# FFN input turned as fp32 halves and scaled out of PSUM, with VectorE's clips ahead of the product of their slot

## The reference

```
x = x + tanh(g_ffn) * FFN(layernorm(x))
FFN(x):
  scale = sigmoid(clip_x) * max|x| / 127          # one number for the whole tensor
  xq    = clip(round(x / scale), -128, 127) * scale
  gate  = xq @ wq(w_gate).T ;  up = xq @ wq(w_up).T     # 704 columns each, weights quantised by row
  h     = silu(gate) * up
  h     = clip(round(h / s2), -128, 127) * s2     # s2 from max|h|, again one number
  return h @ wq(w_down).T
```

## Time and profile before

| what | us |
|---|---|
| median of 3 runs | 591.95 (591.29 to 592.18) |
| profiled execution | 591.61 |
| its span | 589.7 |
| PE busy | 561.8 (95%) |
| DVE busy | 534.1 (91%) |
| ACT busy | 444.0 (75%) |
| POOL busy | 241.7 (41%) |

### The profile page before, as it was taken

The page is one execution under the profiler, slowest core; times in us unless marked ns, Lnnn a source line. Parts: engine busy times, 40 slices in busy tenths (PEclk is TensorE's granted clock), DMA queues, the critical chain, the costliest instruction groups (busy, mean ns, idle before and its releaser), DMA issues. The chain is left out here.

```text
span 589.7 us, 18094 instructions
## 1 busy us (share of the span) xinstructions
PE 561.8 (95%) x6585; PEld 262.7 (45%) x6590; DVE 534.1 (91%) x690; ACT 444.0 (75%) x871; POOL 241.7 (41%) x366
## 2 busy tenths in 40 slices
PE   8999999998999999999999999999999999888985
PEld 4555655233434444444444444444444433433364
DVE  4999999999999999999999899899899885799988
ACT  2667776277787897897897897897797762887694
POOL 3799998702211344562333224214215211555400
PEclk9999999999999999999999999999999999999999
DMA  7579873432122212221221231132121000000024
GB/s 278 195 254 338 283 225 132 144 97 86 56 73 75 76 55 75 79 62 57 80 79 54 66 95 54 54 90 72 54 79 33 2 2 0 2 1 1 0 108 179
DMA packets 29902, 55.21 MB, mean 94 GB/s; under 512 B 5544, under 2 KB 19752, under 8 KB 29864
## 3 DMA queue, kind: packets, MB, share of 16 engines
q1 hardware_dynamic: 29864, 54.71, 28.9%
HBM read 37.62 MB, written 16.78 MB: 92 GB/s over the span
## 5 line engine op out<-in xcount | busy, mean ns | idle before, releaser
L929 ACT ACTIVATE prob<-st_ps 128x512 f32<-128x512 f32 x512 | 280.6, 597 | 61.7 <-PE st_ps L787 54.4
L787 PE MATMUL st_ps<-q,k 98*32 98x512 bf16 x2048 | 178.5, 380 | 1.9 <-ACT prob L929 1.9
L989 DVE TENSOR_REDUCE negm<-xT_ps 128x2 f32<-128x1024 f32 x128 | 154.4, 1206 | 7.3 <-PE xT_ps L339 6.8
L989 DVE TENSOR_REDUCE negm<-v_ps 128x2 f32<-128x1024 f32 x128 | 154.2, 1205 | 3.8 <-PE v_ps L339 3.8
L811 PE MATMUL pv_ps<-prob,v_u 128*32 128x512 f32 x1024 | 132.6, 592 | 0.6 <-ACT prob L929 0.3
L787 PEld LDWEIGHTS st_ps<-q,k 98*32 98x32 bf16 x2048 | 57.3, 95 | 90.5 <-ACT prob L929 33.7
L1181 POOL TENSOR_TENSOR msplit<-negm,onesf 128x16 bf16<-128x16 f32 x32 | 7.1, 221 | 205.9 <-DVE negm L989 205.9
L339 PE MATMUL xT_ps<-k,q 96*32 96x512 bf16 x1024 | 78.5, 379 | 1.1 <-DVE negm L989 1.0
L339 PE MATMUL v_ps<-k,q 96*32 96x512 bf16 x1024 | 78.1, 380 | 1.3 <-DVE negm L989 0.9
L339 PEld LDWEIGHTS xT_ps<-k,q 96*32 96x32 bf16 x1024 | 27.1, 96 | 36.4 <-issue 13.2
L811 PEld LDWEIGHTS pv_ps<-prob,v_u 128*32 128x32 f32 x1024 | 31.2, 110 | 26.8 <-issue 2.8
(11 more groups left out here) (155 smaller groups left out, 782.3 us busy)
## 6 DMA issues: line engine op xcount, KB each, us to landing
qk_parts<-parts SPq DMA_DIRECT2D x32, 384.0 KB, 3.2
k<-qk_parts SPq DMA_DIRECT2D x32, 192.0 KB
q<-qk_parts SPq DMA_DIRECT2D x32, 192.0 KB
ctx<-in_ctxT SPq DMA_DIRECT2D x8, 512.0 KB, 4.6
X<-in_x SPq DMA_DIRECT2D x8, 512.0 KB, 6.2
k<-qk_parts SPq DMA_DIRECT2D x32, 128.0 KB
q<-qk_parts SPq DMA_DIRECT2D x32, 128.0 KB
out<-X SPq DMA_DIRECT2D x7, 512.0 KB, 2.6
```

Source lines behind the costliest of these rows:

```text
L787: last = nc.tensor.matmul(score_bank(i)[lo:lo + COLS, :], k6[g][:, h, kt * P + lo:kt * P + lo + COLS], q6[g][:, h, :], start=True, stop=True)
L929: nc.scalar.activation(prob[kt % 2][:, h, :], score_bank(HPU * kt + h)[:], ACT.Exp, scale=SCALE).then_inc(exp_done, 1)
L989: nc.vector.tensor_reduce(negm[g % 2][:, lo:lo + 2], pair[:], op=ALU.max, axis=AX.X, negate=True).then_inc(mx_read, 1)
```

## The change

Each chunk is now transposed before it is scaled: PE turns `V` itself, in fp32, by halves of the 256 values, 4 transposes of 128 x 128 per half into bank 7 (512 fp32, the whole bank). One pass of ACT (half 0) or DVE (half 1) multiplies by 1/scale and writes int16, from PSUM to SBUF; one clip of DVE over both halves, int16 to bf16, writes `xqT` straight. `scale_x` out of SBUF, `keep_chunk` and `xq` are gone. PE turns half 1 of chunk 1 after slot 0, the halves of the next chunk 0 after slots 3 and 6, half 0 of the next chunk 1 after slot 9. ACT scales in slots 3 and 9 behind its copy of up (in slot 9 that is ahead of silu 10); DVE scales ahead of its products of slots 0 and 5 and clips ahead of those of slots 1 and 7. In pair 0 the four halves go to banks 6, 5, 7 and 2, the first two without a wait for the scale; 3 fillers follow where 9 were. On PE the pairs are written out, not a loop.

```diff
-START, END_A, ..., TO_SCALE, TO_DOWN, TO_CLIP, TO_TURN = 8, 2, 2, 10, 24, 9, 17, 10, 4
+START, END_A, ..., TO_SCALE, TO_DOWN, TO_CLIP, TO_TURN = 8, 2, 2, 10, 24, 3, 17, 10, 4
 # PE
-def transpose_first(): ...
-def transpose_chunk(p, k): ...
+def turn(bank, n, h):
+    for t in range(4):
+        last = nc.tensor.transpose(bank[:, t * P:(t + 1) * P], V[:, 4 * n + t, h * P:(h + 1) * P], ident[:])
+    return last
+def turn_first():
+    for k in range(2):
+        if k:
+            pe.wait_ge(gmax_ready, 1)
+        for h in range(KC):
+            last = turn(first_banks[k][h], k, h)
+        last.then_inc(first_turned, 1)
+def turn_half(n, h):
+    if h:
+        pe.wait_ge(x_kept[0], n - 1)
+    elif n == 2:
+        pe.wait_ge(first_kept[1], 2)
+    else:
+        pe.wait_ge(x_kept[1], n - 2)
+    turn(xT_bank, n, h).then_inc(x_turned, 1)
 ...
-                pe.wait_ge(xqT_kept[0], p)          # at slot 0
+            pe.wait_ge(xq_ready, 2 * p + 1)
+        if is_start(p) and s == 2:
+            pe.wait_ge(first_kept[1], 2)
         if s == NI:
-            pe.wait_ge(xqT_kept[1], p + 1)
+            pe.wait_ge(xq_ready, 2 * p + 2)
 ...
-        if s == 1:
-            transpose_chunk(p, 1)
-        if s == 7 and not last_pair(p):
-            transpose_chunk(p + 1, 0)
+        if s == 0 and not is_start(p):
+            turn_half(2 * p + 1, 1)
+        if not last_pair(p):
+            if s in (3, 6):
+                turn_half(2 * p + 2, (s - 3) // 3)
+            if s == 9:
+                turn_half(2 * p + 3, 0)
 spread(0)
+turn_first()
 stay_busy(banks[:, 0, :], TO_SCALE)
-transpose_first()
-over_pairs(pe, body)
+for p in range(PAIRS):
+    body(p)
 # ACT
-        if s == 7 and not last_pair(p):
-            keep_chunk(p + 1)
+        if s in (3, 9) and not last_pair(p):
+            scale_half(2 * p + 2 + s // 9, s // 9)
+def scale_half(n, k):
+    act.wait_ge(x_turned, 2 * n - 3)
+    act.wait_ge(xq_ready, n - 1)
+    nc.scalar.activation(xi[k][:, 0, :], xT_bank, ACT.Copy, scale=ainv[:, 0:1]).then_inc(x_kept[0], 1)
 # DVE
-def scale_x(p, k): ...
-def keep_chunk(p): ...
+def scale_half(n, k):
+    dve.wait_ge(x_turned, 2 * n - 2)
+    nc.vector.tensor_scalar(xi[k][:, 1, :], xT_bank, ainv[:, 0:1], None, ALU.mult).then_inc(x_kept[1], 1)
+def clip_x(n, k):
+    ...                                             # waits for both halves
+    nc.vector.tensor_scalar(xqT[k], xi[k], QMAX, -QMAX - 1.0, ALU.min, ALU.max).then_inc(xq_ready, 1)
 for s, (ck, c) in enumerate(SLOT):
+    if s == 0 and not is_start(p):
+        scale_half(2 * p + 1, 1)
+    if s == 1 and not is_start(p):
+        clip_x(2 * p + 1, 1)
+    if s == 5 and not last_pair(p):
+        scale_half(2 * p + 2, 0)
+    if s == 7 and not last_pair(p):
+        clip_x(2 * p + 2, 0)
     ...                                             # product and maximum of the slot
-    if s == 2:
-        keep_chunk(p)
-    if not last_pair(p):
-        if s in (2, 6):
-            scale_x(p + 1, s // 4)
-        if s in (3, 7):
-            clip_x(p + 1, s // 4)
```

More of the change, by code:

```diff
@@ L343, in build @@
         CONSTS = 5
-        START, END_A, PROLOGUE, TO_PROJECT, TO_FFN, TO_SCALE, TO_DOWN, TO_CLIP, TO_TURN = 8, 2, 2, 10, 24, 9, 17, 10, 4
+        START, END_A, PROLOGUE, TO_PROJECT, TO_FFN, TO_SCALE, TO_DOWN, TO_CLIP, TO_TURN = 8, 2, 2, 10, 24, 3, 17, 10, 4
         with nc.Block() as block:
@@ L1301, in build @@
         sil = [wf_flat[:, 512 * i:512 * (i + 1)] for i in range(UR)]
-        xi = [wf_flat[:, 2048 + 512 * i:2048 + 512 * (i + 1)].bitcast(I16).rearrange("p (t d) -> p t d", t=4) for i in range(2)]
-        xq = [wf_flat[:, 3072 + 512 * i:3072 + 512 * (i + 1)].bitcast(BF16).rearrange("p (t d) -> p t d", t=4) for i in range(2)]
+        xi = [wf_flat[:, 2048 + 512 * i:2048 + 512 * (i + 1)].bitcast(I16).rearrange("p (c t) -> p c t", c=KC) for i in range(2)]
         xqT = [wfq_flat[:, 1024 * i:1024 * (i + 1)].rearrange("p (c t) -> p c t", c=KC) for i in range(2)]
@@ L1313, in build @@
         u_ps = [banks[:, GR + i, :] for i in range(UR)]
-        xqT_ps = banks[:, 7, :].bitcast(BF16).rearrange("p (c t) -> p c t", c=KC)
-        xqT0_ps = [banks[:, 7 - c, 0:256].bitcast(BF16) for c in range(KC)]
+        xT_bank = banks[:, 7, :]
+        first_banks = [[banks[:, i, :] for i in (6, 5)], [banks[:, i, :] for i in (7, 2)]]
         spread_ps = banks[:, 7, 0:P]
@@ L1322, in build @@
         ascale_ready = sem("ascale_ready")
-        xs_ready = sem("xs_ready")
-        xs0_ready = [sem(f"xs0_ready{k}") for k in range(2)]
         xq_ready = sem("xq_ready")
[L1326 to L1330, removed]
+        first_turned = sem("first_turned")
+        first_kept = [sem(f"first_kept{k}") for k in range(2)]
+        x_turned = sem("x_turned")
+        x_kept = [sem(f"x_kept{h}") for h in range(KC)]
         gscale_ready = sem("gscale_ready")
@@ L1385, in spread @@
                     nc.tensor.transpose(spread_ps, amax[:, n:n + 1].broadcast_to([P, P]), ident[:]).then_inc(spread_ready, 1)
[L1387 to L1404, removed]
-                    else:
-                        pe.wait_ge(xqT_kept[0], p)
[L1407 to L1410, removed]
+                def turn(bank, n, h):
[14 more added lines that the diff above has]
+                        pe.wait_ge(first_kept[1], 2)
+                    else:
+                        pe.wait_ge(x_kept[1], n - 2)
+                    turn(xT_bank, n, h).then_inc(x_turned, 1)
                 def body(p):
@@ L1488, in body @@
                             nc.scalar.activation(upb[j % UBR], u_ps[s % UR], ACT.Copy, scale=gscale[:, NIC + c:NIC + c + 1]).then_inc(upb_ready, 1)
-                        if s == 7 and not last_pair(p):
-                            keep_chunk(p + 1)
-                def keep_chunk(p):
-                    act.wait_ge(xqT_ready, 2 * p)
-                    nc.scalar.activation(xqT[0], xqT_ps, ACT.Copy).then_inc(xqT_kept[0], 1)
+                        if s in (3, 9) and not last_pair(p):
[4 more added lines that the diff above has]
+                    nc.scalar.activation(xi[k][:, 0, :], xT_bank, ACT.Copy, scale=ainv[:, 0:1]).then_inc(x_kept[0], 1)
                 def scale_h(m):
@@ L1505, in _ @@
                 act.wait_ge(ascale_ready, 1)
[L1506 to L1509, removed]
+                act.wait_ge(first_turned, 1)
+                nc.scalar.activation(xi[0][:, 1, :], first_banks[0][1], ACT.Copy, scale=ainv[:, 0:1]).then_inc(first_kept[0], 1)
+                act.wait_ge(first_turned, 2)
+                for h in range(KC):
+                    nc.scalar.activation(xi[1][:, h, :], first_banks[1][h], ACT.Copy, scale=ainv[:, 0:1]).then_inc(first_kept[1], 1)
                 act.wait_ge(gscale_ready, 1)
@@ L1526, in scales @@
                     nc.vector.reciprocal(ainv[:, n:n + 1], ascale[:, n:n + 1]).then_inc(ascale_ready, 1)
[L1528 to L1543, removed]
+                def scale_half(n, k):
+                    dve.wait_ge(x_turned, 2 * n - 2)
+                    nc.vector.tensor_scalar(xi[k][:, 1, :], xT_bank, ainv[:, 0:1], None, ALU.mult).then_inc(x_kept[1], 1)
+                def clip_x(n, k):
+                    if isinstance(n, int) and n < 2:
+                        dve.wait_ge(first_kept[k], 2)
+                    else:
+                        for h in range(KC):
+                            dve.wait_ge(x_kept[h], n - 1)
+                    nc.vector.tensor_scalar(xqT[k], xi[k], QMAX, -QMAX - 1.0, ALU.min, ALU.max).then_inc(xq_ready, 1)
                 def largest(p, j):
@@ L1612, in _ @@
                 dve.wait_ge(ascale_ready, 1)
-                nc.vector.tensor_scalar(xi[0][:, 0:2, :], V[:, 0:2, :], ainv[:, 0:1], None, ALU.mult).then_inc(xs0_ready[0], 1)
+                dve.wait_ge(first_turned, 1)
+                nc.vector.tensor_scalar(xi[0][:, 0, :], first_banks[0][0], ainv[:, 0:1], None, ALU.mult).then_inc(first_kept[0], 1)
                 nc.vector.tensor_scalar(gscale[:], wscale[:, 0:2 * NIC], ascale[:, 0:1], None, ALU.mult).then_inc(gscale_ready, 1)
[L1615 to L1620, removed]
+                for k in range(2):
+                    clip_x(k, k)
                 over_pairs(dve, body)
```

## The result

| | before | changed |
|---|---|---|
| median, us | 591.95 | 588.26 (587.94 to 589.7, 5 runs) |
| ratio to before | | 0.9949 [0.9938, 0.9961] |
| the same, taken again | 591.47 | 588.31, 0.9942 [0.9929, 0.9955] |
| profiled execution, us | 591.61 | 589.7 |

The change makes the kernel 3.2 to 3.7 us faster, 0.5 to 0.6%; 588.8 was forecast. The profiled execution of the changed kernel is its slowest of five. Its first block ended 1.1 us later (first maximum of x, `amax`, at 500.54 against 499.40), and from there to the second `amax` it took 54.21 us for 57.22.

A forecast was written before the change was run, and what follows sets the result against it. DVE's own work and a 13.23 us ring of waits bound a middle pair closely. Terms -0.75, -0.5, -2.14, +0.25 sum to -3.15 us: profiled 591.61 to 588.5, plus 0.34 for the median, 588.8; range 587.5 to 591.3.

The forecast's parts named there:

- start: Before the first product: transposes no longer wait for the scale of x; 0.75 us gained.
- pair 0: First pair, with no maxima of a pair before it: set by PE and ACT, 12.99 for 13.52, gain 0.5 us.
- two middle pairs: Slot 10 to slot 10 on DVE: each takes 12.15 us for 13.22, together -2.14.
- last pair: Slot 10 of pair 2 to the second maximum: gains a half and a clip, loses the copy; 13.85 for 13.61, +0.25.
- the ring: Waits round a middle pair, DVE slot 1, copy of chunk 1, PE, ACT, back to slot 1: 13.23 us, gone after the change.
- The half out of PSUM: DVE's scaling of half a chunk, 512 fp32 to int16: taken at the product's pitch, 0.67 us (745 ns busy).
- The bounds of 0.40 and 1.12: Limits in us for DVE's scaling of half a chunk, from a tensor_scalar of 256 fp32 and a maximum over 1024.
- The clip beside POOL: Clip of chunk 1 ahead of DVE's slot 1 waits 0.60 us for POOL's slot 0 product; clip of chunk 0 waits nothing.
- What is late next: Middle pair walked from DVE's slot 10: data for the half ahead of slot 5 at 6.35, DVE there at 6.45.
- The walk: Before the first product: steps added up from the scale to PE's first slot, 0.85 us gained, of which 0.75 was taken.

The follow-up runs named there:

- e3: Kernel before, with only chunk 1's transposes moved to after slot 0 and its copy ahead of slot 1's product on DVE: 590.21 us, ratio 0.9977.
- e2: Changed kernel, with the clip of chunk 1 moved to slot 2 behind both maxima, where the old copy stood: 590.92 us, ratio 0.9991.
- e4: Changed kernel, with PE making each fp32 half of the transposes in the pairs twice: 591.31 us, ratio 0.9999.
- e1: Changed kernel, with DVE's two halves and two clips right behind the product of their slot, not ahead of it: 587.83 us, ratio 0.9935.
- e5: Changed kernel without the three fillers ahead of pair 0: 588.64 us, ratio 0.9955.

## Why the prediction was right

Term by term, forecast and measured from the profile:

| term | forecast | measured |
|---|---|---|
| start | -0.75 | -0.85 (3.65 to 2.80) |
| pair 0 | -0.5 | -0.46 (13.52 to 13.06) |
| two middle pairs | -2.14 | -1.98 (26.44 to 24.46) |
| last pair | +0.25 | +0.28 (13.61 to 13.89) |
| sum | -3.15 | -3.01 |

*Bound before.* Right: DVE's work and the ring stood half a microsecond apart. e3, which takes the copy out of the ring, falls from 13.22 to 12.85, close to DVE's 12.73; e2, with less work but with the ring, stays at 13.18.

*The half out of PSUM.* Taken at 0.75 busy by the product's row; it is 744 ns over six, and no longer beside POOL (0.75 at 522.91, during POOL's product of 522.10 to 523.38). The bounds of 0.40 and 1.12 weren't needed.

*The clip beside POOL.* Right in place and kind. I forecast a wait of 0.60; the clip of chunk 1 has a pitch of 0.80 (517.91 to 518.71) for 0.33, so 0.47, and 0.18 that I had left out lies ahead of it, since the clip needs its own engine's half to be finished (517.06 to 517.91 for 0.67). Together 0.65: two errors that all but cancel, which is luck. In pair 2 the clip's pitch is 0.88 (530.12 to 531.00), together 0.73, which covers the 0.10 by which that pair is longer than 12.15. The clip of chunk 0 met no product.

*What is late next.* I had DVE reach its half ahead of slot 5 with 0.1 to spare, and it did without a stop that the trace names (pair 1 has 1.16 from maximum to half, for 1.12). That this margin is thin is shown by e2 and e4, where PE is later by some 0.9 and DVE stands there for 0.77 and 0.88.

*Pair 0* is PE's and ACT's: DVE waits 0.73 for its half there (510.70), as walked.

*Start.* The walk gave 0.85, and 0.85 is what came; I had taken 0.1 off it for the hand-overs without need. No run tries the start alone: this term is read from the profile.

The weak step is one that the prediction didn't price: how much of the gain hangs on the clip's place. In the expectation of e2 I put the ring at 12.5, 0.4 over the 12.15 of a pair; it is 13.2, 1.0 over. It is the ring that I had named. What I had too small are two of its terms: the clip, which meets a POOL product in that place as well, and the way from PE's slot 5 to silu 10, where ACT now waits for PE.

## What to carry to other kernels

When an engine's work and a ring of waits are nearly as long, price an edit on both: here the order alone gave 0.37 us a pair, the work alone 0.04 and both 1.0. In an in-order queue put the step that another engine waits for ahead of long work that nobody waits for (here the maxima), and look for what else the same engine will soon wait for behind it. When you add up a ring, take each step at what it costs in its new place: the clip's pitch is 0.33 alone and 0.73 to 0.88 beside a POOL product, and taking it at the lower price is one of the two things that put the expectation of e2 off. A step that always begins during such a product can be tried a little later: in e1 the clip stands behind its slot's product, is short again, and the pairs are no longer than in the changed kernel (12.15 and 12.06 for 12.20 and 12.23).

## What the runs showed of the hardware that I had not expected

Sixteen fp32 transposes in a row and 0.52 us of idle time left PE's granted clock at 1.00 with no filler at all (e5). A DVE instruction that waits for the result of the one right ahead of it starts 0.84 to 0.85 us after it, where the pitch is 0.67 without such a wait: the clip behind its half (517.06 to 517.91), and in both kernels the last maximum behind its product (552.65 to 553.50, before 554.52 to 555.37). That is 0.18 us per such pair of neighbours.
